# A graph-attention kernel: masks and the scores' linear part as small products on TensorE, one wider one-hot on VectorE

## The chip, the core and the metric

The kernel runs on one core of one Trainium2 chip. The metric is device time in microseconds (us) for one call. The core has TensorE (PE, matrix products; its loading of weights is listed as PEld), VectorE (DVE), ScalarE (ACT), GpSimd (POOL) and SyncE (SP, which here only issues DMA transfers). Each engine runs its own instructions in order and waits on semaphores for the others.

## What is computed

The reference is two layers of a GATv2 graph network on 3125 nodes of 128 features with 100000 edges, sorted by destination, followed by a residual and a layer norm. The core of a layer is:

```
h = layer_norm(x)
xl = h @ Wl + bl ; xr = h @ Wr + br          # two heads of 128
e = leaky_relu(xl[src] + xr[dst], 0.2)       # per edge
score = sum(e * att)                          # per edge and head
alpha = softmax of score over the edges with the same dst
out = segment_sum(xl[src] * alpha, dst)
x = x + out @ proj_W + proj_b
x = x + gelu(layer_norm(x) @ W1 + b1) @ W2 + b2
```

## The kernel before

**Units and steps.** The edges are cut into 391 units of 256 edges (UE; K = 2 halves of 128). Since they are sorted by destination, the destinations of a unit lie in a window of 32 nodes (W). Two units (M = 2) make a step; a layer has 196 steps, and then a tail of node work. `edge_pass` is run once per layer for these inputs. A layer's loops are written out in full: each engine has a loop over the step number i, and in round i it works on several steps at different stages.

**The stages of a unit.** GpSimd gathers the rows `xl[src]` with two indirect DMAs per unit (L973) into `rows`, a ring of 20 units; it may run ahead until `z_ready` holds it (units up to three steps ahead). A row holds, per head, 128 features, a one, and the linear part of the score, which is the slope times the dot product of the features with `att` (column D + 1, sign turned). SyncE loads the 32 destination rows of the window as three bf16 pieces (`xrw`, 96 partitions), and for four units at a time `relb`, the destinations relative to the window, copied to 96 partitions (L987). VectorE makes the one-hot `oh` from `relb` (L1305, `one_hot`). TensorE, in `project`, forms z = xl[src] + xr[dst] for both heads: four transposes of the gathered rows (L1090) and two bf16 products of `xrw` and `oh` (L1093). ScalarE writes the positive part `lz` (L1188). TensorE, in `score`, puts the scores of a unit in a bank with 128 partitions (half, head, window node) by 128 edges: first `base`, transposed (L1069), then four products of `att_w` (one head's vector repeated in 32 columns) and `lz` (L1074).

**`base` and `diff`.** A score counts only where the partition's window node is the edge's own destination. VectorE forms per half unit `diff` (L1313, `differ`): 1 where an edge's destination, `cyc_t` (modulo 32, one value per edge and partition), is not the window node in `row_no`. Then per unit `base` = `diff` x 2^100 + the linear part of the gathered row (L1357, `bases`), which waits for the gathered rows. So a foreign edge has a score of 2^100, and the later minimum and exponential (of minus the score) leave it out.

**After the scores.** ScalarE copies a step's scores to `hold_s` (L1259). VectorE takes the minimum (`lowest`, L1327 to L1346), ScalarE the exponential (L1265), TensorE transposes it (L1179), ScalarE copies it to `wgt` (L1200), TensorE forms the weighted sums of the rows (L1163, sixteen instructions on 32 columns for a step), and VectorE adds these to the running sums `acc` (L1436). `sums` of the next step may not start before VectorE has added those of the last one (semaphore `added`).

**Order.** In round i TensorE does the sums of step i - 6, scores of step i - 1 (first unit), project of step i (first unit), the transposes of the exponentials, scores and node work, project (second unit). VectorE does the adds of step i - 7, node work, `lowest` of step i - 3, `bases` of step i, `one_hot` and `differ` of step i + 1, and more node work (L1525 to L1554). The node work of a tile of 128 nodes (projection, norms, GELU network, next layer's projections) is spread over some twenty rounds, and a tile comes every eight rounds.

**Setup.** `setup` loads the lists, checks their order, and makes the tables: VectorE's chain of linked operations ends with the five that make `cyc_t` (L419 to L423) from a transposed copy of the destinations; ScalarE squares the node features (L439) after VectorE's means. GpSimd casts the lists (L324, L325) and clears `acc` (L326).

## Time and profile before

| | |
|---|---|
| Median of three runs | 2283.58 us (2282.32 to 2284.36) |
| Profiled execution: time, span of its instructions | 2276.5 us, 2274.8 us |
| Busy: PE, PEld | 1820.8 us (80%), 1285.0 us (56%) |
| Busy: DVE, ACT, POOL | 1806.9 us (79%), 1368.8 us (60%), 1573.6 us (69%) |
| Mean granted TensorE clock | 0.933 of full |
| DMA moved | 320.66 MB, mean 141 GB/s |

The span runs from the first to the last instruction of the profiled execution. A line such as "L973 POOL DMA_INDIRECT" is line 973 of the kernel on GpSimd. In a row in order of time the first two numbers are start and duration in us, xN says that N equal instructions are merged, and the brackets give the idle time of the engine ahead of it and what ended it; "issue" means that nothing recorded ended it.

### The profile page before, as it was taken

The numbers are of one execution on the slowest core, as the hardware profiler recorded it, in microseconds if no ns is written. First come the engines' busy times: TensorE is split into PE (matmuls) and PEld (weight loads), VectorE is DVE, ScalarE is ACT, GpSimd is POOL, SyncE is SP. The second block draws the span as 40 slices with busy tenths as digits, with TensorE's granted clock in tenths as the row PEclk, the third lists the DMA queues.
The fourth block names the chain that finished last, engine by engine and source line by source line (L and its number), as shares of the span: only waits on it lengthen the run. The fifth ranks groups of instructions, "written<-read, shape, count | busy, mean of one in ns | idle before, by whom it ended". The sixth has DMA issues, their size and how long they took to land. (4 is left out here: it accounts for less than half of the span.)

```text
span 2274.8 us, 76766 instructions
## 1 busy us (share of the span) xinstructions
PE 1820.8 (80%) x22500; PEld 1285.0 (56%) x22500; DVE 1806.9 (79%) x8130; ACT 1368.8 (60%) x3471; POOL 1573.6 (69%) x1663
## 2 busy tenths in 40 slices
PE   2478888888888888888864788888878888888884
PEld 1145566665665665665642565665656656566663
DVE  6757888888888888888854788888888888888874
ACT  3444666666666666666652466666666666666664
POOL 2677777777777777777505777777777777777750
PEclk6878999999999999999976999999999999999995
DMA  4455556556556556555404555555555555555540
GB/s 105 157 158 145 150 152 157 154 150 156 150 150 161 155 146 158 149 152 153 110 23 132 150 146 147 150 152 150 150 147 155 151 149 149 148 154 151 149 109 9
DMA packets 227679, 320.66 MB, mean 141 GB/s; under 512 B 47889, under 2 KB 157574, under 8 KB 227270
## 3 DMA queue, kind: packets, MB, share of 16 engines
q0 software_dynamic: 75072, 208.30, 36.1%
q1 hardware_dynamic: 152198, 107.47, 15.9%
q8 instruction: 187, 3.06, 0.6%
q14 instruction: 222, 1.82, 0.3%
HBM read 295.61 MB, written 19.99 MB: 139 GB/s over the span
## 5 line engine op out<-in xcount | busy, mean ns | idle before, releaser
L973 POOL DMA_INDIRECT rows<-table,src_t x1564 | 1521.0, 973 | 495.1 <-issue 453.4
L1188 ACT ACTIVATE lz<-psum 128x512 f32<-128x512 f32 x782 | 465.6, 595 | 377.6 <-PE psum L1093 189.9
L1090 PE MATMUL psum<-ident,rows 128*128 128x128 f32 x3128 | 529.9, 294 | 56.7 <-DMA rows<-table,src_t 56.3
L1265 ACT ACTIVATE ex<-hold_s,peak 128x128 f32<-128x128 f32 x782 | 272.1, 396 | 410.4 <-DVE peak L1346 409.5
L1163 PE MATMUL psum<-rows,wgt 128*32 128x129 f32 x6256 | 260.8, 284 | 277.6 <-DVE acc L1436 277.0
L1090 PEld LDWEIGHTS psum<-ident,rows 128*128 128x128 f32 x3128 | 351.4, 146 | 210.2 <-issue 140.9
L1436 DVE SCALAR_TENSOR_TENSOR acc<-acc,keep,psum 128x129 f32 x782 | 272.5, 348 | 190.9 <-issue 115.7
L1163 PEld LDWEIGHTS psum<-rows,wgt 128*32 128x32 f32 x6256 | 159.3, 111 | 364.8 <-issue 216.9
L1074 PE MATMUL psum<-lz,att_w 128*32 128x128 f32 x6256 | 345.4, 294 | 0.0
L1093 PE MATMUL psum<-oh,xrw 96*128 96x256 bf16 x1564 | 312.9, 282 | 0.0
L1313 DVE TENSOR_SCALAR diff<-row_no,cyc_t 128x64 bf16<-128x64 f32 x1564 | 290.8, 258 | 0.0
L1357 DVE SCALAR_TENSOR_TENSOR base<-diff,rows 128x128 f32<-128x128 bf16 x782 | 204.0, 293 | 83.2 <-DMA rows<-table,src_t 69.7
L1069 PE MATMUL psum<-ident,base 128*128 128x128 f32 x782 | 241.7, 309 | 0.0
L1305 DVE TENSOR_SCALAR oh<-relb,win_col 96x256 bf16<-96x256 int16 x782 | 195.0, 300 | 6.5 <-DMA relb<-rel_d 5.2
L1074 PEld LDWEIGHTS psum<-lz,att_w 128*32 128x32 f32 x6256 | 125.5, 110 | 120.5 <-issue 76.4
L1179 PE MATMUL psum<-ident,ex 128*128 128x128 f32 x782 | 157.9, 284 | 11.6 <-ACT wgt L1200 11.5
L1093 PEld LDWEIGHTS psum<-oh,xrw 96*128 96x128 bf16 x1564 | 159.9, 102 | 11.6
L1327 DVE TENSOR_REDUCE low<-hold_s 128x2 f32<-128x256 f32 x392 | 161.9, 413 | 0.9 <-issue 0.5
L1130 PE MATMUL psum<-stg,sel 128*32 128x129 f32 x2400 | 160.7, 281 | 1.9 <-DVE xrf L1494 0.9
L1069 PEld LDWEIGHTS psum<-ident,base 128*128 128x128 f32 x782 | 112.5, 144 | 79.7 <-issue 75.2
L1130 PEld LDWEIGHTS psum<-stg,sel 128*32 128x32 f32 x2400 | 142.5, 112 | 6.0 <-issue 2.2
L1259 ACT COPY hold_s<-psum 128x256 f32<-128x256 f32 x392 | 145.1, 370 | 0.0
(253 smaller groups left out, 2130.8 us busy)
## 6 DMA issues: line engine op xcount, KB each, us to landing
xrw<-xr_split SPq DMA_DIRECT2D x782, 48.0 KB
relb<-rel_d SPq DMA_DIRECT2D x194, 192.0 KB
rows<-table,src_t POOLq DMA_INDIRECT x1564
xr_split<-split SPq DMA_DIRECT2D x50, 192.0 KB, 1.9
table<-row SPq DMA_DIRECT2D x50, 130.0 KB, 2.0
x_mid<-x SPq DMA_DIRECT2D x25, 64.0 KB
xo<-x_mid SPq DMA_DIRECT2D x25, 64.0 KB
xo<-in_x_dram SPq DMA_DIRECT2D x24, 64.0 KB
```

The source lines that it names most:

```text
L973: pool.indirect_dma_start(rows[:, u % ROWS, t, :, :].rearrange("p h c -> p (h c)"), None, s["tables"][layer][0:NP, :], bass.IndirectOffset ...
L1069: pe.matmul(out, base[:, u % (2 * M), :, :].rearrange("p c w -> p (c w)"), s["ident"][:, :], is_transpose=True, start=True, stop=False, sk ...
L1074: m = pe.matmul(out[o:o + W, :], w["att_w"][:, h * W:h * W + W], lz[:, u % M, h * UE + t * P:h * UE + t * P + P], start=False, stop=True, ...
L1090: pe.matmul(z[:, o:o + P], rows[:, u % ROWS, t, h, 0:D], s["ident"][:, :], is_transpose=True, start=(h == 0 and t == 0), stop=False, skip_ ...
L1093: m = pe.matmul(z[:, h * UE:h * UE + UE], xrw[:, place(u), h * D:h * D + D], oh[:, u % (2 * M), :], start=False, stop=(h == H - 1), skip_g ...
L1130: mm = pe.matmul(bank(t)[m * W:m * W + W, h * (D + 1):h * (D + 1) + D + 1], s["sel"][:, h, c, :], stg[t % 2][:, 2 * m + c, :], start=(c == 0),
L1163: m = pe.matmul(sum_bank(i - 6)[o:o + W, c:c + D + 1], wgt[:, (u + 1) % (2 * M), o:o + W], rows[:, u % ROWS, t, h, 0:D + 1], start=True, s ...
L1188: act.activation(lz[:, u % M, :], ps[u % M][:, :], ACT.Relu).then_inc(lz_ready, 1)
L1265: m = act.activation(ex[:, (u + 1) % (2 * M), :], hold_s[:, place(u), :], ACT.Exp, bias=peak[:, place(u + 1):place(u + 1) + 1], scale=-1.0)
L1313: m = v.tensor_scalar(diff[:, u % (2 * M) * K + t, :], s["row_no"][:, :], s["cyc_t"][:, u * K + t:u * K + t + 1], None, ALU.not_equal)
L1357: m = v.scalar_tensor_tensor(base[:, u % (2 * M), :, :], diff[:, o:o + K, :].rearrange("p t (h w) -> p (t h) w", h=H), BIG, rows[:, u % RO ...
L1436: m = v.scalar_tensor_tensor(a, a, s["keep"][:, u:u + 1], sum_bank(i - 7)[:, c:c + D + 1], ALU.mult, ALU.add)
```

## The change

The setup makes no transposed `cyc_t`. It makes `cyc_h`, the same values (destination modulo 32) in the layout of the units, as int16, and SyncE writes them to a DRAM table `cyc_d` beside `rel_d`. In the edge pass `relb` and `oh` get 128 partitions: 0 to 95 as before, 96 to 127 hold the modulo-32 destination and are compared with the window node of the partition. The one-hot operation gets a second scalar, `less`, which is 0 on partitions 0 to 95 and 1 on 96 to 127, so that these hold 0 for the edge's own node and -1 elsewhere. `oh` has 3M instead of 2M places. `differ` and `bases` are gone. In `score` the linear part comes from four products of the gathered column (repeated 32 times as the stationary operand) with the identity, and the mask from two products of `mask_w` (-2^100 on partition 96 + w in columns w and 32 + w) with `oh`. These stand ahead of the wait for `lz_ready`.

```diff
 # edge_pass, SyncE
-                sp.dma_start(relb[:, RELS * c:RELS * c + n, :].rearrange("p k e -> p (k e)"),
+                sp.dma_start(relb[0:3 * W, RELS * c:RELS * c + n, :].rearrange("p k e -> p (k e)"),
                              s["rel_d"][i * UE:(i + n) * UE].partition_broadcast(3 * W)).then_inc(rel_in[c], 16)
+                sp.dma_start(relb[3 * W:P, RELS * c:RELS * c + n, :].rearrange("p k e -> p (k e)"),
+                             s["cyc_d"][i * UE:(i + n) * UE].partition_broadcast(W)).then_inc(rel_in[c], 16)
 # edge_pass, TensorE, score(u)
+                if u % M == 0:
+                    hold(pe, held, g - 1)
+                for t in range(K):
+                    for h in range(H):
+                        o = t * HW + h * W
+                        pe.matmul(out[o:o + W, :], rows[:, u % ROWS, t, h, D + 1:RC].to_broadcast([P, W]), s["ident"][:, :],
+                                  start=True, stop=False, skip_group_check=True)
+                for t in range(K):
+                    pe.matmul(out[t * HW:t * HW + HW, :], s["mask_w"][:, :], oh[:, u % (3 * M), t * P:t * P + P],
+                              start=False, stop=False, skip_group_check=True)
                 pe.wait_ge(lz_ready, u + 1)
-                if u % M == 0:
-                    pe.wait_ge(base_ready, g + 1)
-                    hold(pe, held, g - 1)
-                pe.matmul(out, base[:, u % (2 * M), :, :].rearrange("p c w -> p (c w)"), s["ident"][:, :],
-                          is_transpose=True, start=True, stop=False, skip_group_check=True)
 # edge_pass, VectorE
-                    m = v.tensor_scalar(oh[:, u % (2 * M), :], relb[:, u % RING, :], s["win_col"][0:3 * W, 0:1], None,
-                                        ALU.is_equal)
+                    m = v.tensor_scalar(oh[:, u % (3 * M), :], relb[:, u % RING, :], s["win_col"][:, 0:1],
+                                        s["less"][:, 0:1], ALU.is_equal, ALU.subtract)
-            def differ(g):
-...
-            def bases(i):
-...
                 if of_step(i + 1):
-                    hold(v, z_ready, (i - 1) * M + M)
+                    hold(v, score_ready, i - 1)
                     one_hot(i + 1)
-                    hold(v, base_ready, i)
-                    differ(i + 1)
 # setup, VectorE
+            link(v.tensor_scalar(cyc_i[:, :, :], dst_u[:, :, :], PAD + W - 1, None, ALU.bitwise_and))
             link(v.tensor_reduce(ends[:, 1, :], low_f[:, :, :], AX, ALU.max))
             v.tensor_copy(ends[:, 0, :], dst_f[:, :, 0:1].rearrange("p j a -> p (j a)")).then_inc(ends_ready, 1)
+            link(v.tensor_copy(cyc_f[:, :, :], cyc_i[:, :, :]))
+            link(v.tensor_tensor(cyc_f[:, :, :], dst_f[:, :, :], cyc_f[:, :, :], ALU.subtract))
...
             m.then_inc(rel_ready, 1)
+            v.scalar_tensor_tensor(cyc_h[:, :, :], cyc_f[:, :, :], neg_reg[:, 0:1], dst_f[:, :, :], ALU.mult, ALU.add
+                                   ).then_inc(cyc_ready, 1)
```

In the setup there go also: three loads of the destinations for the transposed copy, GpSimd's cast of it (L325), seven of TensorE's fourteen transposes with ScalarE's copies, and the five operations L419 to L423. GpSimd gets six small operations for `less` and `mask_w`. The state `row_no` goes, with one GpSimd copy at the start of each layer.

## Rows read from the trace of the kernel before

**Rows 1.** The chain that ended last, share of the span by engine and line.
```profile
POOL rows L973 16%; DMA rows<-table,src_t 3%; PE psum L1090 2%; DVE acc L1436 2%; DVEq L1367 1%; PE psum L1074 1%; PE psum L1163 1%; PE psum L1130 1%; DVE diff L1313 1%; PE psum L1093 1%; DVE oh L1305 1%; PE psum L1147 1%; PE psum L1069 1%; DVE low L1327 1%; DVE base L1357 0%
```
**Rows 2.** Groups by form: count, busy us, mean ns, idle before, who ended it.
```profile
L973 POOL DMA_INDIRECT rows<-table,src_t x1564 | 1521.0, 973 | 495.1 <-issue 453.4 <-PE psum L1093 38.0 <-POOLq L129 3.7
...
L1313 DVE TENSOR_SCALAR diff<-row_no,cyc_t 128x64 bf16<-128x64 f32 x1564 | 290.8, 258 | 0.0
...
L1357 DVE SCALAR_TENSOR_TENSOR base<-diff,rows 128x128 f32<-128x128 bf16 x782 | 204.0, 293 | 83.2 <-DMA rows<-table,src_t 69.7 <-issue 0.3
L1305 DVE TENSOR_SCALAR oh<-relb,win_col 96x256 bf16<-96x256 int16 x782 | 195.0, 300 | 6.5 <-DMA relb<-rel_d 5.2 <-PE psum L1093 1.1
```
**Rows 3.** Two stretches: PE, PEld, DVE, ACT, POOL busy (count), clock, DMA, GB/s.
```profile
640.00:1100.00 460.00, 393.44 (x5033) 280.30 (x5035) 389.23 (x1782) 299.72 (x759) 344.60 (x353) 0.98 0.59 153
...
1400.00:2200.00 800.00, 684.91 (x8895) 492.25 (x8892) 663.92 (x3041) 513.59 (x1295) 608.95 (x628) 0.97 0.56 150
```
**Rows 4.** Waits from 640 to 1100 us: total us, times, longest.
```profile
PE psum L1163 <- DVE acc L1436: 65.7, 62, 1.9
```
**Rows 5.** Waits from 1400 to 2200 us.
```profile
PE psum L1163 <- DVE acc L1436: 108.4, 94, 1.8
```
**Rows 6.** One ordinary gather in order of time.
```profile
892.45 0.95 POOL L973 DMA_INDIRECT rows<-table,src_t  x1 [0.30 <-issue]
```
**Rows 7.** A long gather and VectorE beside it, in order of time.
```profile
1434.86 0.72 DVE L1313 TENSOR_SCALAR diff<-row_no,cyc_t 128x64 bf16<-128x64 f32 x4
1435.13 1.88 POOL L973 DMA_INDIRECT rows<-table,src_t  x1 [0.30 <-issue]
1435.50 0.68 DVE L1549 SCALAR_TENSOR_TENSOR ge<-arg,am 128x512 f32<-128x512 f32 x1
```
**Rows 8.** TensorE from 895 to 901 us, in order of time.
```profile
895.83 0.41 PEld L1163 LDWEIGHTS psum<-rows,wgt 128*32 128x32 f32 x16 [1.11 <-ACT wgt L1200]
...
896.44 0.14 PEld L1069 LDWEIGHTS psum<-ident,base 128*128 128x128 f32 x1 [0.20 <-issue]
...
896.70 0.16 PEld L1074 LDWEIGHTS psum<-lz,att_w 128*32 128x32 f32 x8
...
897.05 0.42 PEld L1090 LDWEIGHTS psum<-ident,rows 128*128 128x128 f32 x4 [0.20 <-issue]
...
897.44 0.21 PEld L1093 LDWEIGHTS psum<-oh,xrw 96*128 96x128 bf16 x2
...
897.66 0.25 PEld L1179 LDWEIGHTS psum<-ident,ex 128*128 128x128 f32 x2
...
900.88 0.65 PE L1163 MATMUL psum<-rows,wgt 128*32 128x129 f32 x16 [1.45 <-DVE acc L1436]
```
**Rows 9.** First and last gather and last copy of scores, of each layer.
```profile
109.65 1.18 POOL L973 DMA_INDIRECT rows<-table,src_t  x1 [3.93 <-issue]
...
1121.81 0.95 POOL L973 DMA_INDIRECT rows<-table,src_t  x1 [0.30 <-issue]
...
1141.07 0.27 ACT L1259 COPY hold_s<-psum 128x128 f32<-128x128 f32 x1
...
1209.14 0.97 POOL L973 DMA_INDIRECT rows<-table,src_t  x1 [3.74 <-POOLq L129]
...
2203.51 0.95 POOL L973 DMA_INDIRECT rows<-table,src_t  x1 [0.30 <-issue]
...
2215.34 0.27 ACT L1259 COPY hold_s<-psum 128x128 f32<-128x128 f32 x1
```
**Rows 10.** Setup, in order of time.
```profile
16.36 1.05 POOL L325 CAST dst_df<-dst_d 128x896 f32<-128x896 int32 x1
16.65 4.57 DVE L361 CAST win_f<-first_i 128x391 f32<-128x391 int32 x1
...
44.16 1.15 DVE L423 SCALAR_TENSOR_TENSOR cyc_t<-cyc_f,neg_reg,dst_t 128x896 f32<-128x896 f32 x1
...
46.44 0.19 ACT L439 ACTIVATION_READ_ACCUMULATOR psum<-xs,neg_mean  x1
```

More of the change, by code:

```diff
@@ L70, in gnn @@
     rel_d = nc.dram_tensor("rel_d", (UJ * P * UE,), I16, kind="Internal").ap()
+    cyc_d = nc.dram_tensor("cyc_d", (UJ * P * UE,), I16, kind="Internal").ap()
     with ExitStack() as ctx:
@@ L81, in gnn @@
         win_col0 = sb("win_col0", [P, 1], F32)
[L82 to L84 removed]
+        less = sb("less", [P, 1], F32)
+        mask_w = sb("mask_w", [P, HW], BF16)
         sel = sb("sel", [P, H, 3, W], F32)
@@ L160, in gnn @@
         scratch(setup, wts, given, dict(x=x, src=src, dst=dst, rel_d=rel_d, ident=ident, ones=ones, src_t=src_t,
-                            win_col0=win_col0,  cyc_t=cyc_t, row_no0=row_no0, sel=sel, fresh=fresh, keep=keep,
+                            win_col0=win_col0, cyc_d=cyc_d, less=less, mask_w=mask_w, sel=sel, fresh=fresh, keep=keep,
                             at_x0=at_x0, at_s0=at_s0, at_a0=at_a0, tab_s0=tab_s0, tile_no=tile_no, gen=gen, sign=sign, nm=nm,
@@ L168, in gnn @@
         st = dict(ident=ident, ones=ones, xs=xs, sums=sums, neg_mean=neg_mean, var=var, rstd=rstd,
-                  eps_t=eps_t, tables=tables, xr_splits=xr_splits, x_mid=x_mid, x=x, out=out, acc=acc, cyc_t=cyc_t,
-                  row_no0=row_no0, row_no=row_no, sel=sel, src_t=src_t, rel_d=rel_d, fresh=fresh, keep=keep,
+                  eps_t=eps_t, tables=tables, xr_splits=xr_splits, x_mid=x_mid, x=x, out=out, acc=acc, cyc_d=cyc_d,
+                  less=less, mask_w=mask_w, sel=sel, src_t=src_t, rel_d=rel_d, fresh=fresh, keep=keep,
                   win_col=win_col, win_col0=win_col0, at_x=at_x, at_x0=at_x0, at_s=at_s, at_s0=at_s0, at_a=at_a,
@@ L301, in _ @@
             const(pool.iota(third_i[:, :], [[0, 1]], base=0, channel_multiplier=171))
-            const(pool.iota(g["row_no0"][:, :], [[0, H], [1, W]], base=0, channel_multiplier=0,
-                            allow_small_or_imprecise_dtypes=True))
+            const(pool.memset(g["less"][0:3 * W, :], 0.0))
+            const(pool.memset(g["less"][3 * W:P, :], 1.0))
+            const(pool.memset(mask_f[:, :], 0.0))
+            for h in range(H):
+                const(pool.affine_select(out=mask_f[3 * W:P, h * W:h * W + W], in_=mask_f[3 * W:P, h * W:h * W + W],
+                                         compare_op=ALU.not_equal, fill=-BIG, base=0, pattern=[[-1, W]],
+                                         channel_multiplier=1))
+            const(pool.tensor_copy(g["mask_w"][:, :], mask_f[:, :]))
             const(pool.memset(g["sel"][:, :, :, :], 0.0))
@@ L429, in _ @@
                            ).then_inc(order_ready, 1)
-            for j in range(2 * TJ):
+            for j in range(TJ):
                 act.wait_ge(turned, j + 1)
-                to = src_t[:, j, :] if j < TJ else dst_t[:, (j - TJ) * P:(j - TJ) * P + P]
-                act.copy(to, ps[3 + j % 2][:, 0:P]).then_inc(copied, 1)
+                act.copy(src_t[:, j, :], ps[3 + j % 2][:, 0:P]).then_inc(copied, 1)
             act.wait_ge(averaged, 1)
@@ L871, in edge_pass @@
     rows = sb("rows", [P, ROWS, K, H, RC], F32)
-    relb = sb("relb", [3 * W, RING, UE], I16)
-    oh = sb("oh", [3 * W, 2 * M, UE], BF16)
+    relb = sb("relb", [P, RING, UE], I16)
+    oh = sb("oh", [P, 3 * M, UE], BF16)
     xrw = sb("xrw", [3 * W, 4 * M, HD], BF16)
     lz = sb("lz", [P, M, H * UE], F32)
-    diff = sb("diff", [P, 2 * M * K, HW], BF16)
-    base = sb("base", [P, 2 * M, K * H, W], F32)
     hold_s = sb("hold_s", [P, 4 * M, P], F32)
@@ L1347, in lowest @@
                 m.then_inc(max_ready, 1)
-            def bases(i):
-                new = of_step(i)
-                for u in new:
-                    v.wait_ge(rows_in[u % ROWS], (u // ROWS + 1) * (16 * K))
-                    v.wait_ge(diff_ready, i + 1)
-                    hold(v, score_ready, i - 1)
-                    o = u % (2 * M) * K
-                    m = v.scalar_tensor_tensor(base[:, u % (2 * M), :, :],
-                                               diff[:, o:o + K, :].rearrange("p t (h w) -> p (t h) w", h=H), BIG,
-                                               rows[:, u % ROWS, :, :, :].rearrange("p t h c -> p (t h) c"
-                                                                                   )[:, :, D + 1:RC
-                                                                                     ].to_broadcast([P, K * H, W]),
-                                               ALU.mult, ALU.add)
-                m.then_inc(base_ready, 1)
             def slots_of(b):
@@ L1503, in _ @@
                     lowest(i - 3)
-                if of_step(i):
-                    bases(i)
                 if not last:
```

89 lines of the change are left out of this document (34 added, 55 removed).

## The prediction

> **What bounds the kernel now.** I read the page's chain first, then the groups, then the busy time and the waits of two stretches (one per layer), then single steps in order of time, and last the two ends of each layer and the setup. The chain that ended last runs most often through GpSimd's gathers and is named after no other line as much [rows 1]. The groups say how: 1564 gathers of 973 ns, with 495.1 us of idle time before them, of which 453.4 us have no releaser and only 38.0 us wait for TensorE [rows 2]. One gather in order of time is 0.95 us long with 0.30 us of issue ahead of it [rows 6]: 1.25 us, four to a step (two units of edges), so a step can't be shorter than 5.00 us. From the first to the last gather, layer 0 takes 1121.81 - 109.65 = 1012.2 us and layer 1 takes 2203.51 - 1209.14 = 994.4 us [rows 9]. Over 781/4 = 195.25 steps that is 5.18 and 5.09 us a step: 36 and 18 us above the floor. Everything that a faster VectorE can give back lies in this excess of 54 us, and in the backlog at the end of a layer: the last scores are copied out 19.3 us after the last gather in layer 0 and 11.8 us after it in layer 1 [rows 9]. So in layer 0 the other engines are behind GpSimd by as much as the buffers allow, in layer 1 hardly.
>
> Two things make the excess. First, in layer 0's later part the loop of the other engines is slower than GpSimd. TensorE waits at its sums (L1163) for VectorE's adds, 65.7 us in a stretch of 460 us and 108.4 us in one of 800 us [rows 4, 5]. The gathers in these stretches (353 and 628, four to a step) give 88.25 and 157 steps [rows 3], so a step is 5.21 and 5.10 us, and TensorE without that wait needs 4.47 and 4.40 us. VectorE is the one that is late: TensorE waited 1.45 us for it at 900.88 [rows 8]. Second, some gathers are stretched: that of 1435.13 lasts 1.88 us instead of 0.95 and runs beside the mask operations of L1313 and then L1549, which ends at 1436.18 [rows 7]. A normal gather needs another 0.8 us or so after the point where it was let go, which fits an end at 1437.01.
>
> Where the row shows GpSimd held until an operation with two SBUF inputs ends [rows 7], the Trainium skill (SBUF — State Buffer, Who interferes with whom) says that VectorE and GpSimd share a port pair under an exclusive lock, and that an operation with two SBUF inputs contends with a GpSimd instruction that reads SBUF. The gather reads its row numbers there. By that rule, taking `base` and `diff` away shortens the runs of locking operations but leaves L1549, L1545, L1542 and L1554; the sum below would lose no term by it.
>
> **The change, part by part.** *VectorE.* Four `diff` and two `base` operations leave each step: 290.8/391 = 0.74 us and 204.0/391 = 0.52 us [rows 2]. The one-hot gets 128 partitions for 96 and a second scalar; the trace has no such form. At least it costs what it does, 300 ns a piece; at most it runs at the pace of `base`, 293 ns for half as many elements [rows 2], so 0.59 us, 0.6 us more a step. I take today's price, since type, length and kind of operation are those of today's row. VectorE gets 1.26 us a step lighter, 0.66 us at the least, and no longer stands still for the gathered rows. It stops being the late engine either way; what is late next is TensorE or GpSimd.
>
> *TensorE.* Prices from one step in order of time, start of loading to start of loading [rows 8]. L1163 (sixteen instructions on 32 columns) 0.61 us; L1069 0.26; L1074 (eight of the same kind) 0.35; L1090 (four transposes) 0.39, so 0.10 each; L1093 (two of 256 columns) 0.22. L1163 less L1074 makes eight instructions 0.26 us, which leaves 0.09 us in L1074 for the change to the full width behind it; L1069 less one transpose leaves 0.16. So a change of width costs 0.09 to 0.16 us, 0.13 taken, and eight instructions 0.22 to 0.26, 0.24 taken. The new block of a unit is the four linear products (eight instructions, the shape of L1074), two bf16 mask products of 128 columns on 64-wide halves (half of L1093's 0.22 at most, a quarter if the halves overlap: 0.08 taken), and one transpose less. I count 32 to 64 wide as a change too, since both kinds that the rows have (32 to full, full to 32) cost one. Changes per step up to L1074's products: today 3 (sums to L1069, L1069 to L1074 twice), then 5 (into and out of the 64-wide products twice, and from the full width into the second unit's block). Sum: 2 x (0.24 + 0.08) - 2 x 0.10 + 2 x 0.13 = +0.70 us a step. Lower end: quarter price, and 32 to 64 wide costs nothing, so two changes fewer than today: 2 x (0.22 + 0.055) - 0.20 - 2 x 0.16 = +0.03. Upper end: the linear products at L1074's whole 0.35, the masks at L1093's 0.22 plus a change of 0.16, less L1069's 0.26: 2 x 0.47 = +0.94.
>
> No row has 64-wide products, so whether going between 32 and 64 wide costs a change is open here. The Trainium skill (TensorEngine Tiling (Array Packing), Key Properties) says that changing the tiling mode drains TensorE and that 128x64 and 128x32 are different modes. This speaks against the change: by the rule it is +0.70 rather than near zero.
>
> With 0.70 TensorE needs 5.17 and 5.10 us a step. Its mean clock there was 0.98 and 0.97 [rows 3]; as the levels are 2.4 and 1.2 GHz, that is 4 and 6% of the time at the lower one, worth 0.09 and 0.13 us a step. A TensorE that hardly waits should keep the upper level, so 5.08 to 5.17 in layer 0 and 4.97 to 5.10 in layer 1. That is level with GpSimd, at 5.00 plus what is left of the stretching (0.05 to 0.1). I take 5.09 over layer 0 (its first third is bound by GpSimd) and 5.07 over layer 1: -0.09 x 195 = -18 us and -0.02 x 195 = -5 us. Backlog at the ends: layer 0 stays near its 19 us (-1), layer 1 goes from 12 to about 15 us (+3).
>
> *SyncE and DMA.* One more issue per four units, for 32 more partitions: a third more bytes of `relb`. The engines' share was 0.59 and 0.56 [rows 3] and SyncE runs ahead; the lists wait for z_ready as before. 0 us; without that cover the gathers would land late, but they have 10 us. The waits that change (the one-hot waits for the scores of two steps back, already waited for by `bases`; the scores no longer wait for `base`) are not later than today's: 0.
>
> *Setup.* The five operations that go from the end of VectorE's chain ended at 45.31 us, before ScalarE's squares at 46.63 [rows 10], so they were hidden: 0. What counts is when VectorE reaches the squares' input: L361 stood 4.57 us beside GpSimd's casts and memset [rows 10], of which the cast of 1.05 us goes. The new integer mask ahead of `ends` (0.7 us like its neighbours) hides in the same stall. With three fewer loads ahead of the node list it may be 2.5 us. With a GpSimd copy less at each reset: -2 us (0 to -4).
>
> Sum: -18 - 5 - 1 + 3 - 2 = -23 us on the profiled execution's 2276.5 us (span 2274.8, 1.7 us around it), 2253.5. The median of the runs shown is 7.1 us above that execution: 2260.6 us.
>
> **Rivals.** *A, TensorE's additions are cheap* (32 to 64 wide costs nothing, or the products fill its 0.7 us of waiting): TensorE needs 4.5 us, GpSimd alone bounds both layers at 5.07: -22 and -5, the backlog of layer 0 falls to layer 1's 12 us (-7), setup -2: 2247.6 us. For it: the wait of [rows 4, 5] lies right where the new products begin. Against: the width changes seen in [rows 8].
>
> *B, the wait moves* from the adds to another partner (ScalarE's table loads, the copies), and the remaining locking operations stretch as many gathers as now: within 4 us of 2283.6. For it: (973 - 950) ns x 1564 = 36 of the 54 us of excess are stretched gathers [rows 2, 6], and L1549 stays. Against: the late waits all name VectorE's adds.
>
> *C, slower: TensorE becomes the bound* in both layers. Place: the four width changes and eight more fp32 instructions in `score`. Price: +0.94 us, so 5.32 and 5.21 us a step at the full clock: +0.13 x 195 = +25, +0.12 x 195 = +23, backlog of layer 1 +8, setup -2: +54, 2337.6 us. It decides from about +0.8 us a step on. For it: my own price is only 0.1 short of that. Against: every single row is taken at its highest there. The tiling rule named above points this way too.
>
> **How the numbers follow.** A change below 0.2% (4.6 us) can't be told from none. Forecast 0.40, A 0.27, B 0.12, C 0.21. Faster: forecast, A and a little of B, 0.69; same 0.10; slower 0.21. Range: down to A with somewhat less stretching, 2243; up to the middle of C, 2308 (a price of +0.87).
>
> **What would show it.** Right: `base` and `diff` gone, VectorE's busy share down by some 20 points, TensorE's up to about 90%, the waits of L1163 for the adds nearly gone, the time between gathers 5.05 to 5.1 us a step in both layers. Of the price: the time from the start of L1163's loading to L1074's, 0.87 us today, 1.1 to 1.2 then for the first unit. Wrong: gathers released by TensorE (L1093) hundreds of times (C); L1163 still waiting 0.7 us a step (A or B, told apart by the stretched gathers); a one-hot above 0.4 us.

## The result, and the profile after

The changed kernel takes 2228.13 us (median of four runs, 2225.96 to 2230.27) against 2283.97 us: a ratio of 0.9756 (95% interval 0.9739 to 0.9773), 55.8 us less. The forecast was 23 us less: the right direction, and less than half of the size. The profiled execution took 2225.96 us (span 2224.3), 50.5 us less than that of before. The medians lie 7.5 us above the profiled execution before and 2.2 us above it after, which makes up the other 5 us.

Groups of the changed kernel: count, busy us, mean ns, idle time before them and who ended it.

```profile
PE 1979.0 (89%) x29531; PEld 1384.5 (62%) x29531; DVE 1440.9 (65%) x5781; ACT 1371.8 (62%) x3464; POOL 1544.2 (69%) x1664
...
L969 POOL DMA_INDIRECT rows<-table,src_t x1564 | 1492.0, 954 | 483.8 <-issue 460.6 <-PE psum L1096 19.5 <-POOLq L129 3.7
...
L1068 PE MATMUL psum<-ident,rows 128*32 128x128 f32 x6256 | 329.6, 281 | 0.0
L1166 PE MATMUL psum<-rows,wgt 128*32 128x129 f32 x6256 | 257.6, 282 | 26.5 <-DVE acc L1412 20.5
L1308 DVE TENSOR_SCALAR oh<-relb,win_col,less 128x256 bf16<-128x256 int16 x782 | 244.7, 360 | 54.0 <-PE psum L1077 31.6
...
L1071 PE MATMUL psum<-oh,mask_w 128*64 128x128 bf16 x1564 | 193.7, 244 | 0.0
```

The gathers' mean fell from 973 to 954 ns [rows 2]. Of their idle time 19.5 us are still put down to TensorE (38.0 before), but in 64 gaps of at most 0.3 us, which is the ordinary time between two gathers: real waits for TensorE are gone. The sums (L1166) wait 20.5 us for VectorE's adds in the whole run. Before, it was 277.0 us:

```profile
L1163 PE MATMUL psum<-rows,wgt 128*32 128x129 f32 x6256 | 260.8, 284 | 277.6 <-DVE acc L1436 277.0
```

First and last gather and last copy of scores of each layer, answering to [rows 9]:

```profile
107.28 1.18 POOL L969 DMA_INDIRECT rows<-table,src_t  x1 [3.94 <-issue]
1091.73 0.94 POOL L969 DMA_INDIRECT rows<-table,src_t  x1 [0.30 <-issue]
1104.13 0.27 ACT L1262 COPY hold_s<-psum 128x128 f32<-128x128 f32 x1
1171.18 0.97 POOL L969 DMA_INDIRECT rows<-table,src_t  x1 [3.74 <-POOLq L129]
2152.69 1.19 POOL L969 DMA_INDIRECT rows<-table,src_t  x1 [0.30 <-issue]
2164.10 0.27 ACT L1262 COPY hold_s<-psum 128x128 f32<-128x128 f32 x1
```

Layer 0's gathers now take 1091.73 - 107.28 = 984.5 us (5.042 us a step; before 5.184), layer 1's 2152.69 - 1171.18 = 981.5 us (5.027; before 5.093). So the gain splits into: setup -2.4; gathers of layer 0 -27.7; backlog behind them -6.9 (19.3 to 12.4); between the layers -1.0; gathers of layer 1 -12.9; backlog -0.4; the rest +0.7. That is -50.6 us.

Against the floor of 5.00 us a step the gathers' excess can be read one by one. "Waiting" is the idle time ahead of the gathers less 0.30 us each, "stretching" their durations less 0.95 us each, both summed over all gathers of a layer: layer 0 had 12.0 us of waiting and 22.0 us of stretching before, 0.9 and 5.4 us after; layer 1 0.5 and 15.6 us before, 0.7 and 2.7 us after. So layer 1's gain is all from gathers that are no longer stretched; layer 0's from these and from the waits.

Two stretches of the changed kernel, one per layer; columns as in [rows 3]:

```profile
640.00:1100.00 460.00, 445.76 (x6874) 316.32 (x6873) 317.52 (x1296) 311.95 (x792) 343.41 (x359) 1.00 0.61 161
1400.00:2150.00 750.00, 715.35 (x11152) 509.42 (x11151) 497.12 (x2005) 494.67 (x1232) 568.04 (x597) 0.99 0.59 159
```

VectorE's busy time fell from 389 to 318 us of 460, TensorE's rose from 393 to 446. TensorE's granted clock rose from 0.98 and 0.97 to 1.00 and 0.99: busy for 97% of the first stretch instead of 86%, it stood at its upper level of 2.4 GHz practically throughout.

TensorE's loading of weights in one step of the changed kernel, answering to [rows 8]:

```profile
893.93 0.41 PEld L1166 LDWEIGHTS psum<-rows,wgt 128*32 128x32 f32 x16 [0.41 <-issue]
894.29 0.27 PEld L1068 LDWEIGHTS psum<-ident,rows 128*32 128x32 f32 x8
894.76 0.11 PEld L1071 LDWEIGHTS psum<-oh,mask_w 128*64 128x64 bf16 x2 [0.20 <-issue]
894.93 0.16 PEld L1077 LDWEIGHTS psum<-lz,att_w 128*32 128x32 f32 x8
...
895.90 0.25 PEld L1182 LDWEIGHTS psum<-ident,ex 128*128 128x128 f32 x2
896.32 0.16 PEld L1068 LDWEIGHTS psum<-ident,rows 128*32 128x32 f32 x8 [0.17 <-issue]
896.67 0.11 PEld L1071 LDWEIGHTS psum<-oh,mask_w 128*64 128x64 bf16 x2 [0.20 <-issue]
896.85 0.16 PEld L1077 LDWEIGHTS psum<-lz,att_w 128*32 128x32 f32 x8
```

From the sums to the first unit's last products (L1077) it is 894.93 - 893.93 = 1.00 us, before 896.70 - 895.83 = 0.87 [rows 8]. For the second unit it is 896.85 - 895.90 = 0.95 us; the same pieces took 898.19 - 897.66 = 0.53 us before [rows 8], by this row of before:

```profile
898.19 0.16 PEld L1074 LDWEIGHTS psum<-lz,att_w 128*32 128x32 f32 x8 [0.17 <-issue]
```

So the change costs TensorE 0.13 + 0.42 = 0.55 us a step, not 0.70. The medians over all steps of both traces say 0.11 + 0.42.

### The profile page after: what moved, and what is told of

Read it like the earlier page. It is cut to its first block and busy times, and to the rows that moved or that the text cites. A ratio compares the mean times of both kernels' runs of the same rounds, so it can differ in the third digit from the quotient of the medians.

```text
span 2224.3 us, 87495 instructions
## 1 busy us (share of the span) xinstructions
PE 1979.0 (89%) x29531; PEld 1384.5 (62%) x29531; DVE 1440.9 (65%) x5781; ACT 1371.8 (62%) x3464; POOL 1544.2 (69%) x1664
## 5 line engine op out<-in xcount | busy, mean ns | idle before, releaser
L969 POOL DMA_INDIRECT rows<-table,src_t x1564 | 1492.0, 954 | 483.8 <-issue 460.6
L1093 PE MATMUL psum<-ident,rows 128*128 128x128 f32 x3128 | 514.0, 288 | 104.8 <-DMA rows<-table,src_t 103.4
L1093 PEld LDWEIGHTS psum<-ident,rows 128*128 128x128 f32 x3128 | 340.4, 143 | 259.0 <-DMA rows<-table,src_t 143.2
L1077 PE MATMUL psum<-lz,att_w 128*32 128x128 f32 x6256 | 336.1, 287 | 0.0
L1068 PE MATMUL psum<-ident,rows 128*32 128x128 f32 x6256 | 329.6, 281 | 0.0
L1096 PE MATMUL psum<-oh,xrw 96*128 96x256 bf16 x1564 | 303.9, 275 | 0.0
L1166 PE MATMUL psum<-rows,wgt 128*32 128x129 f32 x6256 | 257.6, 282 | 26.5 <-DVE acc L1412 20.5
L1308 DVE TENSOR_SCALAR oh<-relb,win_col,less 128x256 bf16<-128x256 int16 x782 | 244.7, 360 | 54.0 <-PE psum L1077 31.6
L1166 PEld LDWEIGHTS psum<-rows,wgt 128*32 128x32 f32 x6256 | 152.6, 110 | 107.0 <-issue 87.3
L1068 PEld LDWEIGHTS psum<-ident,rows 128*32 128x32 f32 x6256 | 158.1, 109 | 69.4 <-issue 69.4
L1071 PE MATMUL psum<-oh,mask_w 128*64 128x128 bf16 x1564 | 193.7, 244 | 0.0
L1071 PEld LDWEIGHTS psum<-oh,mask_w 128*64 128x64 bf16 x1564 | 85.8, 106 | 157.8 <-issue 157.8
L1077 PEld LDWEIGHTS psum<-lz,att_w 128*32 128x32 f32 x6256 | 123.7, 108 | 53.4
```

Of the source, the lines that this page charges most:

```text
L969: pool.indirect_dma_start(rows[:, u % ROWS, t, :, :].rearrange("p h c -> p (h c)"), None, s["tables"][layer][0:NP, :], bass.IndirectOffset ...
L1068: pe.matmul(out[o:o + W, :], rows[:, u % ROWS, t, h, D + 1:RC].to_broadcast([P, W]), s["ident"][:, :], start=True, stop=False, skip_group_ ...
L1071: pe.matmul(out[t * HW:t * HW + HW, :], s["mask_w"][:, :], oh[:, u % (3 * M), t * P:t * P + P], start=False, stop=False, skip_group_check= ...
L1077: m = pe.matmul(out[o:o + W, :], w["att_w"][:, h * W:h * W + W], lz[:, u % M, h * UE + t * P:h * UE + t * P + P], start=False, stop=True, ...
L1093: pe.matmul(z[:, o:o + P], rows[:, u % ROWS, t, h, 0:D], s["ident"][:, :], is_transpose=True, start=(h == 0 and t == 0), stop=False, skip_ ...
L1096: m = pe.matmul(z[:, h * UE:h * UE + UE], xrw[:, place(u), h * D:h * D + D], oh[0:3 * W, u % (3 * M), :], start=False, stop=(h == H - 1), ...
```

## Experiments

Unless said otherwise a kernel is the changed kernel with the edit shown. "Step" is the time from the first to the last gather of a layer by 195.25. Every time is a median, the ratio is to the kernel before on the same chip.

**VectorE's work put back, TensorE's new work kept.** e1 puts four operations of `diff`'s form and length back into each step; they read a constant tile and a constant column, and nobody reads what they write. e2 puts four minima over 32 elements in their place, half as many as the 64 of `diff`. (In the cut below e2's line stands in place of e1's, not behind it.)

```
+                        for t in range(K):
+                            m = v.tensor_scalar(diff[:, u % (2 * M) * K + t, :], rowx[:, :], s["less"][:, 0:1], None,
+                                                ALU.not_equal)          # e1
+                            m = v.tensor_reduce(least[:, k:k + 1], rowx[:, 0:W], AX, ALU.min)   # e2 instead
```

> The changed kernel, with four operations of the form of diff (128x64 bf16 from f32 in SBUF) put back behind the one-hot of each step; nobody reads what they write. TensorE's work is that of the changed kernel. Theory L (the gain is largely fewer stretched gathers, since the operations that hold GpSimd stood in unbroken rows with diff): the gathers' stretching goes from 8 us back to 20 to 35 us, and the time to 2228 + 12 to 27, so 2240 to 2255 us. Theory T (what counted was VectorE's busy time, which paced the loop): VectorE is at about 4.6 us a step, still under GpSimd's 5.0, so the time stays within 4 us of 2228.

> As the last one, but the four operations are reductions of 32 elements (SBUF, one result), which last as long (about 0.16 us from start to start) and which in the kernel before never stood at the end of a stretched gather. Theory L: stretching stays at 8 to 14 us, the time at 2226 to 2236 us, clearly below the run with diff. Theory T: no difference between the two runs; if VectorE's time is what counts, both are slower than 2228 by the same amount.

Measured: e1 2248.79 us, 0.9845 (0.9829 to 0.9862), +20.7 us on the changed kernel; e2 2237.14 us, 0.9791 (0.9775 to 0.9808), +9.0 us, with 3.9 and 5.0 us of stretching. e1's layer 0 went from 5.042 to 5.107 us a step, with 12.4 us of waiting and 6.5 of stretching; its backlog to 18.8 us; layer 1 stayed at 5.030. So theory L's stretching did not come back with these operations (6.5 and 3.6 us), and theory T's time (within 4 us of 2228) is missed too. What came back is a late VectorE, in layer 0 only. That does not yet clear the original `diff`: e1's operations do not hold gathers as the original ones do, as the part on why the prediction was wrong shows.

**TensorE's new work taken out or made lighter.** e3 leaves the linear part and the mask out of the scores, and one transpose of zeros takes their place (as `base`'s did before). e4 forms the masks 32 wide instead of 64, eight instructions for four a step and no change of width.

```
-                    pe.matmul(out[t * HW:t * HW + HW, :], s["mask_w"][:, :], oh[:, u % (3 * M), t * P:t * P + P],
+                    for h in range(H):
+                        o = t * HW + h * W
+                        pe.matmul(out[o:o + W, :], s["mask_w"][:, h * W:h * W + W], oh[:, u % (3 * M), t * P:t * P + P],
```

> The changed kernel without the six added products of a unit: the scores begin with one transpose of a constant zero tile, as long as the one of base. It leaves out the linear part and the mask. It shows what TensorE's added work (measured at about 0.55 us a step by starts of loading) costs. Theory G (GpSimd's gathers bound both layers, and the products are wholly hidden): time within 4 us of 2228, 4 steps of gathers still 5.03 us; backlog at the layers' ends 12.4 and 11.4 us go to about 11. Theory P (TensorE is level with GpSimd and costs something in heavy rounds): 8 to 20 us faster.

> The changed kernel, with the mask as four bf16 products of 32 columns instead of two of 64, so that the scores' products all have the same width. Same result. If going between 32 and 64 wide costs TensorE a change of 0.13 us each way: from the start of loading of the linear products to that of the att_w products 0.53 us becomes 0.25 to 0.35 us, and TensorE needs 0.4 us a step less. If not: 0.5 to 0.55 stays. In time, by theory G: within 4 us of 2228; by theory P: 8 to 15 us faster.

Measured: e3 2229.56 us, 0.9758 (0.9742 to 0.9774); e4 2227.76 us, 0.9752 (0.9736 to 0.9768). Both are the changed kernel's time. So the products cost nothing of the 2228 us that could be told from none: they are hidden. In e4 the second unit's block in order of time, and the stretch of 640 to 1100 us:

```profile
898.38 0.16 PEld L1068 LDWEIGHTS psum<-ident,rows 128*32 128x32 f32 x8 [0.17 <-issue]
898.52 0.12 PEld L1073 LDWEIGHTS psum<-oh,mask_w 128*32 128x32 bf16 x4
898.63 0.19 PEld L1079 LDWEIGHTS psum<-lz,att_w 128*32 128x32 f32 x8
```

```profile
640.00:1100.00 460.00, 411.35 (x7238) 323.90 (x7240) 318.75 (x1297) 312.83 (x791) 345.24 (x360) 0.98 0.61 161
```

From L1068 to the last products it is 0.25 us, where the changed kernel needs 896.85 - 896.32 = 0.53, with two instructions more: going through the 64-wide masks costs 0.28 us a unit more than going through 32-wide ones, and TensorE's busy time falls by 34 us of 460. Over all steps e4's medians from the sums and from the transposes of the exponentials to the last products are 0.69 and 0.66 us, against 0.87 and 0.53 us of the kernel before: with masks of 32 columns the new products cost TensorE nothing more than `base`'s transpose did. The Trainium skill (TensorEngine Tiling (Array Packing), Available Configurations and Key Properties) has 128x64 and 128x32 as different modes and a change of mode as a drain; the 0.28 us agree. The time did not follow, since TensorE was not late.

**VectorE's old amount of work back.** e8b only makes VectorE wait for the gathered rows as `bases` did; e9b has e1's four operations of `diff`'s form and two of `base`'s form, all on constants; in e10b those of `base`'s form read the gathered rows, with that wait.

```
+                    for u in of_step(i):
+                        v.wait_ge(rows_in[u % ROWS], (u // ROWS + 1) * (16 * K))              # e8b, e10b
+                        m = v.scalar_tensor_tensor(base[:, u % (2 * M), :, :], diffc..., BIG, # e9b, e10b
+                                                   crow or rows..., ALU.mult, ALU.add)
+                            m = v.tensor_scalar(diff[:, u % (2 * M) * K + t, :], rowx[:, :], ...) # e9b, e10b
```

> The kernel of the earlier run of this name again (there the kernel before took 2904 us beside it, and TensorE stood still between instructions for which it waited for nothing). With the kernel before near 2284 us: theory W, stretching of layer 1 from 3 back to 10 to 16 us and 2236 to 2245 us; theory T, within 4 us of 2228 and 3 to 8 us of stretching a layer.

> Again, under the same condition. Four operations as diff gave +20 us (2249) and a late VectorE in layer 0 alone, so theory T for diff and base both: layer 0 at 5.2 to 5.3 us a step with a backlog of 19 us, layer 1 at 5.05 to 5.15; 2270 to 2300 us. Stretching in layer 1 under 8 us by theory W.

> Again, under the same condition: base reads and waits for the gathered rows. Theory W: 12 to 20 us of stretching in layer 1, 6 us more than in the last run, and the time longer by as much. Theory T: the same time as the last run within 4 us.

Measured: e8b 2232.62 us, 0.9788 (0.9764 to 0.9812); e9b 2276.34 us, 0.9979 (0.9965 to 0.9993); e10b 2285.38 us, 1.0017 (1.0004 to 1.0031). The wait for the rows can't be told from no cost (4.5 us by the times, 7 us by the ratios, and the intervals of e8b and of the changed kernel overlap). With the work, all but 0.2% of the gain is gone in e9b and all of it in e10b, and nearly all of this loss is in layer 0. e9b's busy times, and its first and last gather of each layer:

```profile
PE 1974.5 (87%) x29531; PEld 1384.5 (61%) x29531; DVE 1832.2 (81%) x8125; ACT 1379.0 (61%) x3464; POOL 1554.2 (68%) x1664
```

```profile
107.42 1.18 POOL L977 DMA_INDIRECT rows<-table,src_t  x1 [3.93 <-issue]
1128.92 0.95 POOL L977 DMA_INDIRECT rows<-table,src_t  x1 [0.30 <-issue]
1216.58 0.97 POOL L977 DMA_INDIRECT rows<-table,src_t  x1 [3.73 <-POOLq L129]
2200.11 0.94 POOL L977 DMA_INDIRECT rows<-table,src_t  x1 [0.30 <-issue]
```

Layer 0 needs 1021.5 us (5.232 a step), layer 1 983.5 us (5.037): layer 1 does not feel VectorE at 81%. So e9b is as slow as the kernel before in sum, and not in its parts: layer 0 is 9.3 us longer than before and layer 1 is 10.9 us shorter. In layer 0 the stretching came back in part (13.9 us, e10b 14.7, where the changed kernel has 5.4 and the kernel before 22.0), in layer 1 it did not (4.9 and 4.3). In the stretch of 640 to 1100 us, VectorE's busy time by steps (gathers by four) against the step of the whole layer 0: changed kernel 3.54 and 5.042; e2 3.86 and 5.041; e1 4.17 and 5.107; before 4.41 and 5.184; e9b 4.46 and 5.232; e10b 4.48 and 5.255. In these runs up to some 3.9 us of VectorE a step is free for the gathers, and above it each further 0.1 us comes with 0.02 to 0.04 us more.

**More work on TensorE.** e5b forms the linear part twice in every unit (eight more instructions of L1068's kind, in a block of their own).

> Again, under the same condition. TensorE's need of 4.89 and 4.79 us a step plus 0.48: 5.37 and 5.27, so about 2350 us, with TensorE the releaser of hundreds of gathers. If the products still hide: within 5 us of 2228.

Measured: 2312.15 us, 1.0131 (1.0106 to 1.0155): slower than before. Its chain and its windows:

```profile
PE 36%; issue 3%; ACT 2%; POOL 2%; DVE 2%; DVEq 1%; DMA 1%; SPq 0%; ACTq 0%; POOLq 0%
```

```profile
640.00:1100.00 460.00, 456.71 (x7867) 335.23 (x7866) 301.99 (x1233) 294.36 (x744) 329.54 (x346) 1.00 0.59 157
1400.00:2150.00 750.00, 743.08 (x13062) 551.08 (x13058) 478.44 (x1918) 472.62 (x1186) 550.75 (x579) 1.00 0.59 154
```

TensorE is 99% busy and bounds both layers, at 5.260 and 5.163 us a step. The eight instructions were expected to give 5.37 and 5.27 (about 2350 us): either they or the rest of TensorE's work take some 0.1 us less than was reckoned. So the changed kernel is one such block away from rival C: it was real, and not reached.

**Where layer 1's stretching went.** f2b is e10b without the products (linear part and mask are missing from the scores, a transpose of zeros in their place): in amount of work nearly the kernel before, built from the changed one. f1b is the kernel before with the products of the change added ahead of its scores, overwritten by the transpose of `base`.

```
+                pe.matmul(out, basec[:, :], s["ident"][:, :], is_transpose=True, ...)      # f2b, for the products
...
+                for t in range(K):                                                         # f1b, in the kernel before
+                    for h in range(H):
+                        pe.matmul(out[o:o + W, :], rows[:, u % ROWS, t, h, D + 1:RC].to_broadcast([P, W]), ...)
+                for t in range(K):
+                    pe.matmul(out[t * HW:t * HW + HW, :], maskd[:, :], oh[:, u % (3 * M), t * P:t * P + P], ...)
```

> The changed kernel with all of VectorE's old diff and base operations computed again and waited for (as e10b), and with TensorE's linear and mask products left out (the linear part and the mask are missing from the scores; the base transpose takes their place, as in the kernel before). That is nearly the kernel before, built from the changed one. Theory S (the stretched gathers of layer 1 of the kernel before come from TensorE's shorter scores, which let VectorE's long operations meet the gathers): layer 1 has 12 to 18 us of gather time above 0.95 us a piece, against 4.3 in e10b, and 5.08 us a step; time 2278 to 2288 us. Rival R (they come from something else that the change took away, the layout of buffers or order of issue on VectorE): 3 to 6 us of it and 5.03 us a step, 2268 to 2278 us.

> The kernel before, with all it does, and the products of the change added on TensorE ahead of its scores, with a mask of zeros, their result overwritten by the transpose of base behind them. Theory S: the longer scores take the stretched gathers of layer 1 away: 3 to 6 us above 0.95 us a piece and 5.03 us a step there; layer 0 needs more on TensorE than any kernel with VectorE as the pacer (0.65 us a step on top, so 5.2 to 5.3 us a step); 2280 to 2300 us. Rival R: layer 1 keeps its 15 us and 5.09 us a step or more; 2290 to 2312 us.

Measured: f2b 2286.54 us, 1.003 (1.0021 to 1.004), with 6.2 us of stretching and 5.044 us a step in layer 1. Without the products the stretched gathers of layer 1 do not come back, which speaks against theory S but does not settle it, since f2b has e1's operations and not the original `diff`. Rival R fits on the stretching, while f2b's time is 8 us above its range, since layer 0 needs 5.280 us a step. Against the kernel before its one-hot is the wider one: 359 for 300 ns, 0.12 us a step, where VectorE is the late engine, and the step is 0.10 longer. That this price, hidden in the changed kernel, is what shows here is argued from the two figures only.

f1b took 2382.25 us, 1.0449 (1.0431 to 1.0466), and missed both ranges: 5.450 and 5.310 us a step. Its busy times, the head of its chain and the stretch in layer 1:

```profile
PE 2180.1 (92%) x30320; PEld 1494.9 (63%) x30320; DVE 1806.7 (76%) x8132; ACT 1373.3 (58%) x3471; POOL 1575.8 (66%) x1663
...
PE 32%; DVE 5%; issue 3%; POOL 3%; ACT 2%; DVEq 1%; DMA 0%; SPq 0%; ACTq 0%; POOLq 0%
```

```profile
1400.00:2150.00 750.00, 734.12 (x10736) 514.51 (x10733) 593.25 (x2696) 458.29 (x1148) 536.18 (x560) 1.00 0.53 143
```

734.12 us of 750 busy at the full clock: TensorE bounds both layers. In the same two units it has the change's products and, behind them, a full-width transpose each with two changes of width, which the change saves. So it says nothing on the stretching of a layer that GpSimd bounds, and shows instead what the products cost if the transposes stay: 102 us more than before. It has 32.8 us of stretching in layer 0 and 7.1 us in layer 1, the most of all runs, and beside the kernel before it is the only run near 2280 us with the original `diff`.

**The same on other chips.** Eight runs fell on two chips on which the kernel before itself takes 2904.53 and 2836.58 us. There e5 (e5b's kernel) took 3567.99 us, e8 (e8b's) 3275.44, e9 3297.59, e10 3307.80, against 2904.53; the changed kernel itself (f0) 3211.76, f1 (f1b's) 3292.39, f2 (f2b's) 2843.29 against 2836.58. e7 is the kernel before with `diff` formed in the first two steps only (the mask is a stale one): 2820.14 us, 0.9941 (0.9924 to 0.9957).

> The changed kernel, with the four linear products of a unit done twice (the second time starts the sum anew, so the result is the same). It adds eight instructions on 32 columns per unit and no change of width: 0.24 us, 0.48 us a step. TensorE without waits took 4.89 us a step from 640 to 1100 us and 4.79 us from 1400 to 2150 us in the changed kernel. If TensorE's needs add up so and the bound is whichever of TensorE and GpSimd is longer: 5.37 and 5.27 us a step against 5.04 and 5.03, so +64 and +47 us, and both backlogs go to 19 us (+14): about 2350 us, TensorE the releaser of hundreds of gathers. Rival (the products still hide): within 5 us of 2228.

> The changed kernel, with VectorE waiting for the gathered rows of step i where base waited for them before; nothing else. Theory W (before the change, this wait tied VectorE's long operations to a fixed moment after a gather, and so L1549 and its neighbours met the next gathers at a bad moment): the stretching of layer 1 goes from 3 us back to 10 to 16 us, the time to 2236 to 2245 us. Theory T (VectorE's time alone; there is 1.5 us of slack a step): within 4 us of 2228, stretching 3 to 8 us per layer.

> The changed kernel with VectorE's old work back: four operations as diff and two of the form of base, which read constant tiles and wait for no rows; nobody reads them. So VectorE is at least as heavily loaded as before the change and TensorE as after it. Theory T (VectorE's loop paces layer 0 and nearly paces layer 1): layer 0 at 5.2 to 5.3 us a step, backlog 19 us, layer 1 at 5.1 to 5.2: 2285 to 2310 us. Theory W says of the stretching that it stays small (under 8 us) in layer 1, as the operations are not tied to the rows.

> As the last one, but the operations of the form of base read the gathered rows and wait for them, as before the change. Theory W: stretching in layer 1 of 12 to 20 us, at least 6 us more than in the last run, and the time longer by as much. Theory T: the same time within 4 us, at 2285 to 2310 us, and the same stretching.

> The changed kernel itself, beside the others on one chip: 0.976 of the kernel before, about 2228 us.

> The kernel before, with the six products of a unit added ahead of its base (their sum is started anew by base, so nothing of them is left; the mask operand is zero). VectorE's work is that of the kernel before, TensorE's is one transpose more than the changed kernel's. Theory S (the stretching of a layer that GpSimd bounds depends on when TensorE's scores let VectorE's long operations run): the stretching of layer 1 falls from 15.6 to under 8 us, layer 0 gets longer (TensorE 5.1 us a step beside a late VectorE) by 5 to 15 us: 2275 to 2295 us. Rival (stretching comes from VectorE's operations alone): it stays at 13 to 18 us in layer 1, and the time is 2285 to 2300 us.

> The changed kernel with all of VectorE's old work, base waiting for the rows, and without the six products (a constant tile transposed in their place; it leaves out the linear part and the mask). In work this is nearly the kernel before. Theory S: stretching of layer 1 rises from 4.3 to 12 us or more, time 2275 to 2290 us. Rival (something else of the kernel before, such as the order of waits ahead of the one-hot, made it): it stays under 7 us, time 2268 to 2280 us.

> The kernel before with diff formed for the first two steps alone (later steps use what stands there, so the mask is not the edges' own). VectorE loses 0.65 us a step and keeps base with its wait for rows. Theory T (VectorE's time paces layer 0): layer 0 falls from 1012 to 985 to 995 us, its backlog to 12 to 19 us; layer 1 keeps at least half of its stretching: 2240 to 2260 us. If only both operations together bring it (a threshold): 2270 to 2284 us.

In absolute time all of these are hundreds of microseconds off what was expected; f2's ratio there, 1.003, is that of f2b. On these chips the change makes the kernel slower: f0's ratio is 1.1322 (1.1298 to 1.1345). What the traces show of it stands in the last section. They settle nothing of the disputes above, as their gathers wait for TensorE throughout; e7 is the one run without the original `diff` that is otherwise the kernel before, and its 10.8 us of stretching can be held only against 15.4 us of f1 beside it, which has `diff` but also the products.

## Why the prediction was wrong

**Right.** GpSimd's gathers are the floor; all that VectorE's lighter loop can give lies in their excess and in the backlog. VectorE was the late engine in layer 0: e9b, which puts the work back and keeps the products, loses 48 us of 56, and 44 of them in layer 0 and its backlog. No cost of SyncE's additional issue is to be seen, though no run has it alone; the setup gained 2.4 us for a forecast of 2. TensorE's busy share reached 89%. VectorE's fell by 14 points where I had said some 20: its busy time in the stretch of layer 0 went from 4.41 to 3.54 us a step, 0.87 us less and not 1.26, in part because the wider one-hot takes 360 ns and not 300.

**Failed: the step that made TensorE level with GpSimd.** The price was +0.70 us a step; it measured +0.55, with a change between 32 and 64 wide at about the price that I had given it (0.28 us for the two of a unit, by e4). The first unit's block was to take 1.1 to 1.2 us and took 1.00. With the clock at 1.00, as I had argued, TensorE then needs about 4.47 + 0.55 = 5.02 us in layer 0 at the old clock, less 0.09 for the clock: 4.93, below the gathers' 5.04 instead of 5.08 to 5.17. So the term "5.09 over layer 0" (-18 us) had to be 5.04 (-27.7), and the backlog of layer 0 shrank to 12.4 us as under rival A (-6.9 for -1), and that of layer 1 did not grow (-0.4 for +3). e3 and e4 show that TensorE's price costs nothing in either layer at this size. Its slack is small all the same: 5.04 - 4.93 = 0.1 us a step in layer 0 by this sum, and 0.26 if e5b's 5.260 is taken less the 0.48 us reckoned for its block; e5b and f1b, past it, are slower than before.

**Failed: "what is left of the stretching (0.05 to 0.1)".** I took most of the stretched gathers as lasting, since L1549 and its like stay, and rival A has the same figure, 5.07. Measured: gathers' busy time less 1564 x 0.95 was 1521.0 - 1485.8 = 35.2 us and is 1492.0 - 1485.8 = 6.2 us, 0.02 us a step. That is 29 of the 50.5 us, and the whole of layer 1's gain (-12.9 for -5). With 5.035 for its 5.07 over 390.5 steps, rival A's 2247.6 would have been 2234 us.

What the stretching is, the traces show. Of the 159 gathers of before that last over 1.00 us, 136 end 0.81 to 0.83 us behind the end of a VectorE operation that ran as they began or started just after; of the 64 of the changed kernel it is 59. One of the changed kernel, VectorE's and GpSimd's rows in order of time:

```profile
896.20 0.69 DVE L1521 SCALAR_TENSOR_TENSOR ge<-arg,am 128x512 f32<-128x512 f32 x1
```

```profile
896.35 1.36 POOL L969 DMA_INDIRECT rows<-table,src_t  x1 [0.30 <-issue]
```

L1521 ends at 896.89, the gather at 897.71. It is the operation of [rows 7] under its new line. Counting the gathers over 0.98 us, 37 ended so behind it before, stretched by 12.3 us in sum; after, 13, by 4.3 us, though it runs as often and as long. So the number of meetings changed, and not the rule. The Trainium skill (SBUF — State Buffer, Who interferes with whom) names as contending the operations with two SBUF inputs, and those in a two-port mode, which a `tensor_scalar` can enter. The trace agrees for both kinds: behind the `tensor_tensor` of L1545 ended 20 stretched gathers (3.3 us), behind the `tensor_scalar` of L1542 17 (6.2 us), and behind the one-hot, also a `tensor_scalar`, 17 before (1.1 us) and 40 after (2.3 us).

What a gather meets as it begins tells more than what it ends behind. The gather of [rows 7] begins during a `diff` and is then held through L1549 as well. Gathers that began while an operation named `diff` ran:

| | gathers | over 1.00 us | time above 0.95 us each, in sum |
|---|---|---|---|
| before, original `diff` | 191 | 53 | 19.1 us (of 35.2 of all gathers) |
| f1b, original `diff` | 186 | 74 | 22.9 us |
| e1, same form on constants | 152 | 9 | 3.7 us |
| e9b, e10b, f2b, same form on constants | 221, 217, 204 | 17, 20, 26 | 3.5, 4.5, 7.0 us |

The gather of [rows 7] begins 0.27 us after the first `diff` and 0.37 us ahead of L1549, and lasts 1.88 us. One of e1 stands just so between the same operations (L1534 is L1549's there), and is not held at all:

```profile
1035.87 0.72 DVE L1498 TENSOR_SCALAR diff<-rowx,less 128x64 bf16<-128x64 f32 x4
1036.13 0.95 POOL L974 DMA_INDIRECT rows<-table,src_t  x1 [0.30 <-PE psum L1101]
1036.51 0.68 DVE L1534 SCALAR_TENSOR_TENSOR ge<-arg,am 128x512 f32<-128x512 f32 x1
```

So, counted by where the gathers begin, more than half of the stretching of before lies at the original `diff`, and the operations that e1 and its followers put in its place do not act like it on the gathers. The prediction had named this, that the change shortens the runs of locking operations, and had put it at nothing in the sum. It can be the source of up to 19 of the 29 us (13.6 us in layer 0, 5.5 in layer 1), which is theory L in other words. That is argued and not shown: no run near 2280 us takes the original `diff` away alone or puts it back into the changed kernel. The rest of layer 1's 12.9 us is open as well, and so is why the stand-ins hold so few gathers: the original reads `row_no` and another column of `cyc_t` each time, while they read another tile and one and the same column. The other differences of f2b remain possible: the order of waits on VectorE (the one-hot waits for the scores of two steps back, not for the second half of `project`, and has a third pair of buffers) and the second list from DRAM.

**Of the rivals.** A was the right mechanism (the products are hidden, GpSimd bounds both layers), forecast at 2247.6; the chance of 0.27 should have been the largest. Its first condition (no cost between 32 and 64 wide) is false by e4; its second (the products fill TensorE's idle time) is true. Its 2247.6 is off too, by the same 5.07 for the gathers. B fell: the gathers are no longer held by any engine behind them, and the stretched gathers did not stay. C's place and price were real, and by e5b and f1b it begins at one more block in each unit.

## What to carry to other kernels

When an engine is late only because its loop is long, moving its work to another pays up to that one's own idle time, so count the receiver's need without waits and at the full clock, and treat a sum that comes out level with the floor as undecided until every term is a measured one. Excess over a floor is to be split by rows into waiting and stretching before it is forecast, and the stretching by what the stretched instructions met as they began: when that is an operation that the change removes, its share belongs into the sum. And a stand-in that is to put removed work back must be compared with the original in what it does to its neighbours, and not in form and length alone.

## What the runs showed of the hardware that was not expected

On two chips TensorE stands still between instructions that wait for nothing. f0, the changed kernel, in order of time, and its group of gathers with what released them:

```profile
1903.36 0.22 PE L1071 MATMUL psum<-oh,mask_w 128*64 128x128 bf16 x1 [1.18 <-issue]
1904.81 0.80 PE L1077 MATMUL psum<-lz,att_w 128*32 128x128 f32 x8 [1.24 <-issue]
```

```profile
L969 POOL DMA_INDIRECT rows<-table,src_t x1564 | 1488.6, 952 | 1451.5 <-PE psum L1096 1065.7 <-issue 363.3 <-remote 10.1
```

The gathers wait 1065.7 us for TensorE. The time there follows the number of TensorE's pairs of loading and product: the kernel before (22500 pairs) takes 2836.58 us and f2 (22493) 2843.29; f0 (29531) takes 375 us more for 7031 more pairs, 0.053 us a pair; on the other chip e8 (29531) 371 us more, 0.053, and e5 (35787) 663 us more for 13287, 0.050. Where VectorE's old work is there too it is somewhat more (f1, 30320 pairs: 456 us, 0.058). On the chip of e3 the products cost nothing. That these two chips are slower in bringing instructions to TensorE fits the `issue` in the rows; no run shows it, and a trace of the kernel before on them was not taken. So the change is 2.4% faster where it was first measured, kernels close to it are about as fast on two more chips (e4 0.9752, e8b 0.9788), and on these two it is 13% slower (f0; e8, nearly the changed kernel, 1.1262). There the number of small products goes with the time.
